# Cross attention: two of eight head pairs masked behind the exponentials by GpSimd

## The chip, the core and the metric

The kernel runs on one core of a Trainium2 chip. The metric is the device time of one launch in microseconds (us). The engines are called TensorE (PE in the rows), VectorE (DVE), ScalarE (ACT), GpSimd (POOL) and SyncE (SP, which here only issues transfers).

## The reference

A decoder layer on a batch of 128 sequences with 128 tokens of 256 features: self attention, cross attention over a context of the same shape, and a feed-forward part, each with a layer norm before it and a residual. Both attentions have 16 heads of 16 features. What the change touches is the mask of the cross attention:

```python
scores = jnp.einsum('bhqd,bhkd->bhqk', Q, K) / jnp.sqrt(jnp.float32(D_K))
scores = jnp.where(mask == 0, jnp.float32(1e-09), scores)
attn = jax.nn.softmax(scores, axis=-1)
out = jnp.einsum('bhqk,bhkd->bhqd', attn, V)
```

The mask has ones and zeros for each pair of query and key and is the same for all sequences and heads. A masked key keeps a score of about zero, so it keeps a weight.

## The kernel before

**Jobs and slots.** The batch is cut into 32 groups of 4 sequences (512 tokens). Each group is a self job and later a cross job: 64 jobs. The first six are self jobs, then cross and self jobs alternate (26 of each), and the last six are cross jobs. The program is a row of slots. In slot n every engine works on several jobs at once, each at another stage: job n+2 is normalised, n+1 projected, job n (`s.max`) gets its row maxima and values, job n-1 (`s.exp`) its exponentials and weighted sums, and job n-2 (`s.out`) its output product. Two sets of buffers ("even", "odd") take turns. Inside a slot each engine's order is written out by hand, and semaphores alone join the engines. After the last slot the feed-forward stage runs over the same groups.

**The exponentials of a job.** The 16 heads are 8 pairs. For pair p, `shifted(p)` on TensorE writes the transposed scores less the row's maximum into `exp_bank`; `exps(p)` on ScalarE turns them into `prob` (128 x 1024). `weighted(qd)` on TensorE multiplies the `prob` of pairs 2qd and 2qd+1 with the values; `outputs(b, s.exp, qd)` on VectorE transposes the result, for cross jobs adds the masked keys' part `ue`, and divides by the sum. `prob` has three buffers.

**The mask.** For a cross job, `add_mask` puts a large negative number on the masked places: four matmuls of 512 columns start the bank, and the scores are added to them. It is used for the maxima (`scores(m)` into `score_bank`, `sh.maskB`) and for the exponentials (`shifted(p)`, `sh.maskBT`). So masked places have an exponential of zero, and their true share (score about zero) comes in as `ue`, from sums over the masked keys.

**Order around the change.** On TensorE a slot runs `tile(0..3)` (projections of the next job), `scores(0..7)`, `shifted(0..7)`, `weighted(0..3)`, `products` (output product of an earlier job), `values` and `turn_maxima`, interleaved. `shifted(p)` waits for `exps(p-1)`, since there is one `exp_bank`. `scores(m)` waits for `maximum(m-1)` on VectorE, since there is one `score_bank`. VectorE runs `tile` (the low parts of the projections), `maximum(0..7)`, `outputs(0..2)` and at the end `negate`, for which `turn_maxima` waits. `outputs(3)` falls into the next slot. GpSimd has `low_outputs`, `low_norm`, `residual` and `biased` in a slot, and `low_context` for a cross job; all are subtractions or additions in SBUF.

**Prepared weights.** The feed-forward weights are made ternary and transposed at the start and stay in SBUF (`wfcT`, `wpT`).

## Time and profile before

| | |
|---|---|
| median of 3 runs | 2367.21 us (2365.73 to 2368.36) |
| the profiled execution | 2370.91 us |
| its span | 2369.1 us |
| TensorE busy | 2183.7 us, 92% |
| VectorE busy | 1933.5 us, 82% |
| ScalarE busy | 1596.8 us, 67% |
| GpSimd busy | 1044.4 us, 44% |
| chain that ended last, by engine | TensorE 65%, VectorE 18%, ScalarE 7%, issue 7% |

The span is the time from the first to the last instruction in one profiled execution; its own time lies 1.8 us above it and 3.7 us above the median. Busy shares are means over stages with different limits. The chain is followed back from the last instruction, at each step to what released it.

### The profile page before, as it was taken

Reading aid. Unit: us, or ns where it says so; the run is one execution under the profiler, and the core shown is the slowest. Engines: PE = TensorE matmul, PEld = TensorE weight load, DVE = VectorE, ACT = ScalarE, POOL = GpSimd, SP = SyncE. Lnnn points to the kernel's source line nnn. Section 1 sums busy time; section 2 is a strip of 40 time slices with the busy share of each in tenths; the row PEclk is TensorE's granted clock in tenths of the full one; section 3 lists DMA queues with packets and bytes.
Section 4 is the critical chain, followed back from the end, with each engine's and each line's share of the span. In section 5 each row is a group of like instructions: output and inputs, shape, how many; then the busy total and the mean of one; then the engine's idle time right before and its main releaser. Section 6 shows DMA issues by size and latency. Waiting matters only on the chain.

```text
span 2369.1 us, 70234 instructions
## 1 busy us (share of the span) xinstructions
PE 2183.7 (92%) x29033; PEld 1449.4 (61%) x29033; DVE 1933.5 (82%) x3903; ACT 1596.8 (67%) x2354; POOL 1044.4 (44%) x849
## 2 busy tenths in 40 slices
PE   4689999999999999999999999999967999999999
PEld 2356656656665666566566656655544777777776
DVE  5788888888888888888888888887745788887887
ACT  3377666667666666666666666665535878778786
POOL 2144443454444344444434444454224554555543
PEclk9799999999999999999999999999978999999999
DMA  4567666676666667666666766676422333333332
GB/s 129 117 151 175 156 144 155 145 158 157 157 153 152 155 140 159 157 160 153 154 150 143 153 161 157 159 173 144 89 59 54 84 103 80 97 89 83 103 81 63
DMA packets 472860, 311.01 MB, mean 131 GB/s; under 512 B 288144, under 2 KB 423184, under 8 KB 472592
## 3 DMA queue, kind: packets, MB, share of 16 engines
q1 hardware_dynamic: 469488, 306.80, 55.0%
q8 instruction: 205, 3.36, 0.6%
q10 hardware_dynamic: 3104, 0.34, 0.1%
q14 instruction: 63, 0.52, 0.1%
HBM read 71.65 MB, written 50.33 MB: 51 GB/s over the span
## 4 chain that ended last, share of the span: by engine, by line
PE 65%; DVE 18%; ACT 7%; issue 7%; SPq 1%; DMA 1%; POOL 1%; DVEq 0%; ACTq 0%; POOLq 0%
PE product_bank L1106 14%; PE ybk L1434 9%; PE hbk L1458 9%; PE out_bank L1082 7%; PE tbk L1448 5%; ACT prob L811 4%; PE product_bank L1113 4%; PE score_bank L1030 4%; DVE out_bank L940 4%; PE score_bank L1049 3%; DVE odd_mx L906 3%; PE exp_bank L1067 3%; PE exp_bank L1030 3%; PE exp_bank L1167 3%; DVE att L955 2%
## 5 line engine op out<-in xcount | busy, mean ns | idle before, releaser
L811 ACT ACTIVATE prob<-exp_bank 128x1024 f32<-128x1024 f32 x512 | 523.1, 1022 | 254.6 <-PE exp_bank L1067 246.6
L735 POOL TENSOR_TENSOR xs<-xn,xs 128x1024 f16<-128x1024 f32 x64 | 136.3, 2130 | 638.8 <-ACT xs L835 638.8
L906 DVE TENSOR_REDUCE even_mx<-score_bank 128x8 f32<-128x1024 f32 x256 | 310.5, 1213 | 97.4 <-PE score_bank L1049 97.4
L906 DVE TENSOR_REDUCE odd_mx<-score_bank 128x8 f32<-128x1024 f32 x256 | 310.2, 1212 | 81.0 <-PE score_bank L1049 81.0
L801 ACT ACTIVATE qk<-product_bank,bcol 128x512 f16<-128x512 f32 x256 | 175.9, 687 | 232.0 <-PE product_bank L1106 228.7
L1458 PE MATMUL hbk<-wfcT,ffn_xhl 128*128 128x512 f16 x1024 | 264.5, 382 | 6.3 <-ACT hid L1355 3.4
L1418 DVE SCALAR_TENSOR_TENSOR ghl<-tbk,lnwc,ghl 128x512 f16<-128x512 f32 x256 | 188.0, 735 | 100.3 <-ACT ghl L1349 100.3
L1434 PE MATMUL ybk<-wpT,ghl 128*128 128x256 f16 x2048 | 260.5, 273 | 0.8 <-DVE ffn_y L1403 0.7
L1434 PEld LDWEIGHTS ybk<-wpT,ghl 128*128 128x128 f16 x2048 | 197.8, 98 | 66.1 <-DVE ghl L1418 0.9
L1349 ACT ACTIVATE ghl<-tbk,lnwc 128x512 f16<-128x512 f32 x256 | 174.1, 681 | 68.1 <-PE tbk L1448 68.1
L940 DVE STREAM_TRANSPOSE out_bank<-out_bank 128x512 f32<-128x512 f32 x256 | 183.5, 717 | 24.8 <-PE out_bank L1082 24.7
L912 DVE SCALAR_TENSOR_TENSOR qk<-product_bank,bcol,qk 128x512 f16<-128x512 f32 x256 | 184.2, 740 | 22.4 <-ACT qk L801 22.4
L1030 PE MATMUL exp_bank<-maskBT,pick 64*128 64x512 bf16 x1024 | 156.5, 385 | 45.3 <-ACT prob L811 27.7
L1113 PE MATMUL product_bank<-WT,ahl 128*128 128x256 f16 x1536 | 192.9, 276 | 4.8 <-POOL ahl L735 4.8
L735 POOL TENSOR_TENSOR ahl<-attT,ahl 128x512 f16<-128x512 f32 x128 | 148.6, 1161 | 100.6 <-ACT ahl L816 100.6
L1379 DVE BATCH_NORM_STATS2 hstats<-hid 128x6 f32<-128x512 f32 x256 | 174.1, 680 | 16.5 <-ACT hid L1355 16.4
L1355 ACT ACTIVATE hid<-hbk 128x512 f32<-128x512 f32 x256 | 152.4, 596 | 51.0 <-PE hbk L1458 44.0
L1106 PE MATMUL product_bank<-odd_xhl,WT 128*128 128x512 f16 x732 | 176.0, 384 | 7.6 <-DVE qk L912 5.6
L1113 PEld LDWEIGHTS product_bank<-WT,ahl 128*128 128x128 f16 x1536 | 141.4, 99 | 34.3 <-POOL ahl L735 5.1
L1030 PE MATMUL score_bank<-maskB,pick 64*128 64x512 bf16 x1024 | 154.7, 381 | 6.3 <-DVE even_mx L906 5.6
L1448 PE MATMUL tbk<-ident,hid 128*128 128x128 f32 x1024 | 154.4, 274 | 0.7 <-ACT hid L1355 0.7
L1458 PEld LDWEIGHTS hbk<-wfcT,ffn_xhl 128*128 128x128 f16 x1024 | 98.2, 98 | 75.1 <-ACT hid L1355 5.2
(174 smaller groups left out, 4401.3 us busy)
## 6 DMA issues: line engine op xcount, KB each, us to landing
even_stk<-qk SPq DMA_DIRECT2D x384, 128.0 KB, 2.7
odd_stk<-qk SPq DMA_DIRECT2D x384, 128.0 KB, 2.8
x_scratch<-xn SPq DMA_DIRECT2D x64, 512.0 KB, 4.8
ctx_in<-in_ctx SPq DMA_DIRECT2D x32, 512.0 KB, 4.6
ffn_src<-x_scratch SPq DMA_DIRECT2D x32, 512.0 KB, 3.8
out<-ffn_y SPq DMA_DIRECT2D x32, 512.0 KB, 3.7
odd_src<-in_x SPq DMA_DIRECT2D x29, 512.0 KB, 5.4
even_src<-x_scratch SPq DMA_DIRECT2D x29, 512.0 KB, 5.5
```

The costliest lines, as they stand in the source:

```text
L735: nc.gpsimd.tensor_tensor(out, src, hi, ALU.subtract).then_inc(lo_ready, 1)
L811: act.activation(prob[:, p % 3], ebank[:, :, :], ACT.Exp, scale=EXP_SCALE).then_inc(b.exp_done, 1)
L906: dve.tensor_reduce(a.mx[:, g * H:(g + 1) * H].rearrange("p (r e j) -> p r e j", r=2, e=2)[:, :, eight], sbank[:, :, :].rearrange("p r (j ...
L912: dve.scalar_tensor_tensor(qk[:, 3 * (n // 2), n % 2], pbank[:, n % 2], sh.bcol[:, 2 * s.proj.which + n // 2, n % 2:n % 2 + 1], qk[:, 1 + ...
L940: dve.transpose(obank[:, 1], obank[:, 0]).then_inc(ch.o_turned, 1)
L1030: pe.matmul(bank[:, r].rearrange("p (b s) -> p b s", b=G), sh.pick[rows, h], mask[rows, h].unsqueeze(1).broadcast_to([HALF, G, S]), start= ...
L1106: last = pe.matmul(pbank[:, n % 2].rearrange("p (b s) -> p b s", b=G), sh.WT[:, (s.proj.wq, s.proj.wk)[n // 2], wp, kt, n % 2 * P:(n % 2 + ...
L1113: last = pe.matmul(pbank[:, g // 2, g % 2 * D:(g % 2 + 1) * D], stationary(part, g, kt), sh.WT[:, w, wp, kt, :], start=(k == 0 and kt == 0 ...
L1418: dve.scalar_tensor_tensor(ghl[:, LO, s], tbk[:, TURN_BANK[s]], sh.lnwc[:, s:s + 1], ghl[:, HI, s], ALU.mult, ALU.subtract).then_inc(glo_r ...
L1434: last = pe.matmul(ybk[:, b], ghl[:, part, t, b * S:(b + 1) * S], sh.wpT[:, t], start=(t == 0 and part == HI and b % 2 == 0), stop=(t == F ...
L1448: last = pe.transpose(tbk[:, TURN_BANK[s], b * S:(b + 1) * S], hid[:, 1 - half, b, s * P:(s + 1) * P], sh.ident[:, :])
L1458: last = pe.matmul(hbk[:, s % 2], xhl[:, half, part, s // 2, kt], sh.wfcT[:, kt, s % 2 * HF:(s % 2 + 1) * HF], start=(part == HI and kt == ...
```

## The change

For cross jobs, pairs 0 and 2 (`KEPT`) get no mask on TensorE. ScalarE takes the exponential of all their scores. GpSimd then bounds `prob` above by 3e38 (a masked score may lie over the maximum of the others, and its exponential may overflow) and multiplies it with `keepT`, a table of zeros and ones. `weighted(qd)` also waits for this (`kept`). `prob` gets a fourth buffer, so `exps(4)` and `exps(6)` wait for a weighted sum where `exps(3)`, `exps(5)` and `exps(7)` did.

In slots whose exponentials are of a cross job, `weighted(0)` moves behind `products(0, 1)`, `weighted(1)` behind `products(2, 3)`, and on VectorE `maximum(4)` goes before the outputs of quad 0.

To make room in SBUF, `wfcT` and `wpT` are written to DRAM at the start and read again before the feed-forward stage. Some semaphores of the setup are merged, so that some waits ask for one transfer more.

```diff
+LARGE = 3e38
+KEPT = (0, 2)
...
+        def store_made(sp):
+            sp.wait_ge(fc_out, 2)
+            sp.dma_start(wfc_dram, wfcT[:, :, :].rearrange("p k f -> p (k f)")).then_inc(made_stored, 16)
+            sp.wait_ge(pj_out, 4)
+            sp.dma_start(wp_dram, wpT[:, :, :].rearrange("p t d -> p (t d)")).then_inc(made_stored, 16)
+            sp.wait_ge(made_stored, 32)
...
+            nc.vector.tensor_scalar(sh.keepT[:, :], bank[:, 5, 0:S], -1.0, 1.0, ALU.mult, ALU.add)
...
-        prob = sb("prob", [P, 3, 2, T])
+        prob = sb("prob", [P, 4, 2, T])
...
+            def keep_unmasked(p):
+
+                if s.exp and s.exp.cross and p in KEPT:
+                    pool.wait_ge(b.exp_done, 8 * s.exp.k + p + 1)
+                    tile = prob[:, p % 4].rearrange("p r (b s) -> p (r b) s", s=S)
+                    nc.gpsimd.tensor_scalar(prob[:, p % 4], prob[:, p % 4], LARGE, None, ALU.min).then_inc(bounded, 1)
+                    pool.wait_ge(bounded, len(KEPT) * s.exp.g + KEPT.index(p) + 1)
+                    nc.gpsimd.tensor_tensor(tile, tile, sh.keepT[:, :].unsqueeze(1).broadcast_to([P, 2 * G, S]), ALU.mult).then_inc(kept, 1)
...
             low_outputs(a, s.out, 1)
+            for p in KEPT:
+                keep_unmasked(p)
             low_norm()
...
-                    if p > 2 and p % 2:
-                        act.wait_ge(b.pv_done, 4 * s.exp.k + (p - 3) // 2 + 1)
+                    if p > 3 and p % 2 == 0:
+                        act.wait_ge(b.pv_done, 4 * s.exp.k + (p - 4) // 2 + 1)
...
-            outputs(b, s.exp, 0)
-            maximum(4)
+            if s.exp and s.exp.cross:
+                maximum(4)
+                outputs(b, s.exp, 0)
+            else:
+                outputs(b, s.exp, 0)
+                maximum(4)
...
-                if s.exp.cross:
+                masked = s.exp.cross and p not in KEPT
+                if masked:
                     add_mask(ebank, sh.maskBT)
...
+                if s.exp.cross:
+                    pe.wait_ge(kept, len(KEPT) * s.exp.g + sum(1 for p in KEPT if p < 2 * qd + 2))
...
+            late = s.exp is not None and s.exp.cross
...
-            weighted(0)
+            if not late:
+                weighted(0)
             scores(3)
             shifted(3)
             products(0, 1)
+            if late:
+                weighted(0)
             scores(4)
             shifted(4)
-            weighted(1)
+            if not late:
+                weighted(1)
             scores(5)
             shifted(5)
             products(2, 3)
+            if late:
+                weighted(1)
...
+            sp.dma_start(wfcT[:, :, :].rearrange("p k f -> p (k f)"), wfc_dram).then_inc(made_loaded, 16)
+            sp.dma_start(wpT[:, :, :].rearrange("p t d -> p (t d)"), wp_dram).then_inc(made_loaded, 16)
```

TensorE in a slot with the exponentials of a cross job, from `weighted(0)` in the kernel before (`out_bank<-prob` is a weighted sum, `exp_bank<-maskBT` a mask, `product_bank<-WT,ahl` the products):

```order
L1082 MATMUL out_bank<-prob,even_vals 32x128 x16
L1049 MATMUL score_bank<-odd_stk 128x128 x8
L1030 MATMUL exp_bank<-maskBT,pick 128x512 x4
L1067 MATMUL exp_bank<-even_stk 128x128 x8
L1113 MATMUL product_bank<-WT,ahl 128x256 x12
L1049 MATMUL score_bank<-odd_stk 128x128 x8
L1030 MATMUL exp_bank<-maskBT,pick 128x512 x4
L1067 MATMUL exp_bank<-even_stk 128x128 x8
L1082 MATMUL out_bank<-prob,even_vals 32x128 x16
L1049 MATMUL score_bank<-odd_stk 128x128 x8
L1030 MATMUL exp_bank<-maskBT,pick 128x512 x4
L1067 MATMUL exp_bank<-even_stk 128x128 x8
```

The same place in the changed kernel, from the mask of pair 3 to `weighted(1)`:

```order
L1060 MATMUL exp_bank<-maskBT,pick 128x512 x4
L1098 MATMUL exp_bank<-even_stk 128x128 x8
L1146 MATMUL product_bank<-WT,ahl 128x256 x12
L1115 MATMUL out_bank<-prob,even_vals 32x128 x16
L1079 MATMUL score_bank<-odd_stk 128x128 x8
L1060 MATMUL exp_bank<-maskBT,pick 128x512 x4
L1098 MATMUL exp_bank<-even_stk 128x128 x8
L1079 MATMUL score_bank<-odd_stk 128x128 x8
L1060 MATMUL exp_bank<-maskBT,pick 128x512 x4
L1098 MATMUL exp_bank<-even_stk 128x128 x8
L1146 MATMUL product_bank<-WT,ahl 128x256 x12
L1115 MATMUL out_bank<-prob,even_vals 32x128 x16
```

Both weighted sums now stand behind the twelve product matmuls that followed them.

VectorE in the same slot, from maximum 3 in the kernel before (`odd_mx` is a maximum; the four operations from the transpose to `att` are the outputs of one quad):

```order
L906 TENSOR_REDUCE odd_mx<-score_bank 128x2x4
L940 STREAM_TRANSPOSE out_bank<-out_bank 128x512
L947 TENSOR_TENSOR out_bank<-out_bank,ue 128x16x17
L951 RECIPROCAL rec<-out_bank 128x16
L955 TENSOR_TENSOR att<-out_bank,rec 128x16x16
L906 TENSOR_REDUCE odd_mx<-score_bank 128x2x4 x2
L940 STREAM_TRANSPOSE out_bank<-out_bank 128x512
```

And in the changed kernel:

```order
L932 TENSOR_REDUCE odd_mx<-score_bank 128x2x4 x2
L966 STREAM_TRANSPOSE out_bank<-out_bank 128x512
L973 TENSOR_TENSOR out_bank<-out_bank,ue 128x16x17
L977 RECIPROCAL rec<-out_bank 128x16
L981 TENSOR_TENSOR att<-out_bank,rec 128x16x16
L932 TENSOR_REDUCE odd_mx<-score_bank 128x2x4
L966 STREAM_TRANSPOSE out_bank<-out_bank 128x512
```

Maximum 4 has moved ahead of the outputs of quad 0.

GpSimd in the same slot of the changed kernel:

```order
L750 TENSOR_TENSOR ahl<-attT,ahl 128x512
L786 TENSOR_SCALAR prob<-prob 128x1024
L788 TENSOR_TENSOR prob<-prob,keepT 128x1024
L786 TENSOR_SCALAR prob<-prob 128x1024
L788 TENSOR_TENSOR prob<-prob,keepT 128x1024
L750 TENSOR_TENSOR xs<-xn,xs 128x1024
```

The four operations on `prob` are new; the first and last row followed each other before.

## Rows read from the trace of the kernel before

**Rows 1.** Busy time by stretch, middle of attention: stretch, length, engines, clock, DMA
```profile
260.00:1500.00 1240.00, 1175.09 (x18483) 753.29 (x18486) 1070.41 (x1911) 846.17 (x1146) 556.89 (x456) 1.00 0.67 154
```

**Rows 2.** Timeline, TensorE, one cross slot: start, length, work, idle before
```profile
814.32 2.76 PE L1106 MATMUL product_bank<-even_xhl,WT 128*128 128x512 f16 x12
...
819.74 1.47 PE L1106 MATMUL product_bank<-ctx_hl,WT 128*128 128x512 f16 x6
...
823.09 0.61 PE L1030 MATMUL exp_bank<-maskBT,pick 64*128 64x512 bf16 x4 [0.90 <-ACT prob L811]
823.53 0.39 PE L1067 MATMUL exp_bank<-even_stk 64*128 64x128 f16 x8
823.85 1.08 PE L1082 MATMUL out_bank<-prob,even_vals 128*32 128x128 f32 x32
824.86 0.40 PE L1049 MATMUL score_bank<-odd_stk 64*128 64x128 f16 x8
...
825.85 1.48 PE L1113 MATMUL product_bank<-WT,ahl 128*128 128x256 f16 x12
827.26 0.40 PE L1049 MATMUL score_bank<-odd_stk 64*128 64x128 f16 x8
...
829.59 0.40 PE L1049 MATMUL score_bank<-odd_stk 64*128 64x128 f16 x8 [0.26 <-DVE odd_mx L906]
...
830.57 1.48 PE L1113 MATMUL product_bank<-WT,ahl 128*128 128x256 f16 x12
831.99 0.61 PE L1030 MATMUL exp_bank<-maskBT,pick 64*128 64x512 bf16 x4
...
838.29 0.33 PE L1148 MATMUL score_bank<-ident,odd_negm 128*16 128x128 f16 x3 [0.42 <-DVE odd_negm L969]
```

**Rows 3.** Timeline, ScalarE, the same slot
```profile
819.68 1.02 ACT L811 ACTIVATE prob<-exp_bank 128x1024 f32<-128x1024 f32 x1
...
823.96 1.02 ACT L811 ACTIVATE prob<-exp_bank 128x1024 f32<-128x1024 f32 x1
...
828.36 1.02 ACT L811 ACTIVATE prob<-exp_bank 128x1024 f32<-128x1024 f32 x1 [1.31 <-PE exp_bank L1067]
```

**Rows 4.** Timeline, VectorE, the same slot
```profile
818.94 0.73 DVE L912 SCALAR_TENSOR_TENSOR qk<-product_bank,bcol,qk 128x512 f16<-128x512 f32 x1
...
825.30 1.23 DVE L906 TENSOR_REDUCE odd_mx<-score_bank 128x8 f32<-128x1024 f32 x1 [0.53 <-PE score_bank L1049]
826.44 0.72 DVE L940 STREAM_TRANSPOSE out_bank<-out_bank 128x512 f32<-128x512 f32 x1
...
828.32 1.21 DVE L906 TENSOR_REDUCE odd_mx<-score_bank 128x8 f32<-128x1024 f32 x1
...
831.17 0.72 DVE L940 STREAM_TRANSPOSE out_bank<-out_bank 128x512 f32<-128x512 f32 x1
...
838.01 0.23 DVE L969 TENSOR_TENSOR odd_negm<-odd_mx,mshift 128x64 f16<-128x64 f32 x1
```

**Rows 5.** Timeline, GpSimd, the same slot
```profile
830.40 2.13 POOL L735 TENSOR_TENSOR xs<-xn,xs 128x1024 f16<-128x1024 f32 x1 [10.59 <-ACT xs L835]
```

**Rows 6.** Groups by line and form: count, busy us, mean ns, idle before
```profile
L764 POOL TENSOR_TENSOR odd_xb<-odd_src,boB 128x1024 f32<-128x1024 f32 x32 | 76.0, 2375 | 72.4 <-DVE odd_negm L969 67.5 <-DVE odd_negm L967 4.9
...
L279 POOL TENSOR_SCALAR_AFFINE_SELECT ident<-ident 128x128 f32<-128x128 f32 x1 | 0.3, 297 | 0.2 <-POOL ones L276 0.2
```

**Rows 7.** DMA issues (count, size, us to landing), then SyncE's queue around slot 0
```profile
x_scratch<-xn SPq DMA_DIRECT2D x64, 512.0 KB, 4.8
...
78.51 0.37 SPq L1208 DMA_DIRECT2D ctx_in<-in_ctx  x1
85.89 2.57 SPq L660 DMA_DIRECT2D odd_stk<-qk  x4
```

**Rows 8.** Timeline, the last cross jobs: VectorE, then TensorE
```profile
1658.01 1.40 DVE L920 TENSOR_TENSOR ue<-ew,cntL 128x64 f32<-128x64 f32 x1
...
1661.28 2.25 PE L1106 MATMUL product_bank<-ctx_hl,WT 128*128 128x512 f16 x6 [1.83 <-DVE qk L912]
```

More of the change, by code:

```diff
@@ L67, in __init__ @@
         self.WT = sb("WT", [P, 8, 2, KT, D], F16)
-        self.wfcT = sb("wfcT", [P, KT, F], F16)
-        self.wpT = sb("wpT", [P, FT, D], F16)
         self.bcol = sb("bcol", [P, 4, KT])
@@ L85, in __init__ @@
         self.maskcT = sb("maskcT", [P, S])
+        self.keepT = sb("keepT", [P, S])
         self.cntL = sb("cntL", [P, BLOCKS])
@@ L110, in decoder_layer_kernel @@
         sh = Shared(sb)
-        prep = setup(nc, stack, ins, sh)
+        prep = setup(nc, stack, ins, sh, wfc_dram, wp_dram)
         att = attention(nc, stack, ins, sh, x1_dram, x2_dram, prep)
-        mlp = ffn(nc, stack, sh, x2_dram, out, att)
+        mlp = ffn(nc, stack, sh, x2_dram, out, att, wfc_dram, wp_dram)
         LAST = 2 * NG
@@ L397, in ternary @@
             dve.wait_ge(total_done, 1)
-            nc.vector.tensor_scalar(thr[:, :], bank[:, 0, 0:2], 1.0 / (F * D), GAMMA_EPS, ALU.mult, ALU.add).then_inc(gamma_done, 1)
-            dve.wait_ge(gamma_done, 1)
+            nc.vector.tensor_scalar(thr[:, :], bank[:, 0, 0:2], 1.0 / (F * D), GAMMA_EPS, ALU.mult, ALU.add).then_inc(thr_done, 1)
+            dve.wait_ge(thr_done, 1)
             nc.vector.tensor_scalar(nthr[:, :], thr[:, :], -0.5, None, ALU.mult).then_inc(thr_done, 1)
-            dve.wait_ge(thr_done, 1)
+            dve.wait_ge(thr_done, 2)
             nc.vector.tensor_scalar(thr[:, :], thr[:, :], 0.5, None, ALU.mult).then_inc(thr_done, 1)
-            dve.wait_ge(thr_done, 2)
+            dve.wait_ge(thr_done, 3)
             for n in range(2):
-                wait(dve, tern_done, n)
-                nc.vector.tensor_scalar(neg[:, :], fnat[:, n], nthr[:, n:n + 1], None, ALU.is_lt).then_inc(neg_done, 1)
-                dve.wait_ge(neg_done, n + 1)
+                wait(dve, tern_done, 2 * n)
+                nc.vector.tensor_scalar(neg[:, :], fnat[:, n], nthr[:, n:n + 1], None, ALU.is_lt).then_inc(tern_done, 1)
+                dve.wait_ge(tern_done, 2 * n + 1)
                 nc.vector.scalar_tensor_tensor(fnat[:, n], fnat[:, n], thr[:, n:n + 1], neg[:, :],
@@ L1067, in shifted @@
                         last = pe.matmul(ebank[:, r, g * S:(g + 1) * S], b.stk[rows, s.exp.k % 2, 1, p % 4, p // 4, g * S:(g + 1) * S],
-                                         b.stk[rows, s.exp.k % 2, 0, p % 4, p // 4, g * S:(g + 1) * S], start=not s.exp.cross, stop=True, skip_group_check=True)
+                                         b.stk[rows, s.exp.k % 2, 0, p % 4, p // 4, g * S:(g + 1) * S], start=not masked, stop=True, skip_group_check=True)
                 last.then_inc(b.st_mm, 1)
@@ L1226, in attention, with ffn @@
         return part
-def ffn(nc, program, sh, x2_dram, out, before):
+def ffn(nc, program, sh, x2_dram, out, before, wfc_dram, wp_dram):
     x2_groups = x2_dram.rearrange("(n b) s d -> n s b d", b=G)
@@ L1260, in ffn @@
         held = sb("ffn_held_wait", [P, 2, G + 1])
+        wfcT = sb("wfcT", [P, KT, F], F16)
+        wpT = sb("wpT", [P, FT, D], F16)
         hbk = ps("hbk", [P, 2, HF])
@@ L1433, in second @@
                     for part in (HI, LO):
-                        last = pe.matmul(ybk[:, b], ghl[:, part, t, b * S:(b + 1) * S], sh.wpT[:, t],
+                        last = pe.matmul(ybk[:, b], ghl[:, part, t, b * S:(b + 1) * S], wpT[:, t],
                                          start=(t == 0 and part == HI and b % 2 == 0), stop=(t == FT - 1 and part == LO),
@@ L1454, in pe_body @@
                             pe.wait_ge(x_turned, 16 * (k + 1))
+                            if isinstance(k, int) and k == 0:
+                                pe.wait_ge(made_loaded, 32)
                         wait(pe, hid_ready, 8 * k + s - 1)
```

49 lines of the change are left out of this document (28 added, 21 removed).

## Prediction

> **What bounds the kernel now.** I read the views in this order: busy time by stretch, to find the stage; the timeline of one slot of it, engine by engine, to find which wait ends last; then the groups and transfers that price what is new. In the middle of attention TensorE works 1175.09 of 1240 us at full clock, while GpSimd works 556.89 [rows 1]. So a reader could expect every removed matmul to come off the time. The slot's timeline says otherwise. I take the slot that runs the exponentials of a cross-attention job (TensorE from 814.32 [rows 2]) and write "at 823.09" for a time in that trace. Three places matter.
>
> First, ScalarE sets the pace of the early pairs. Scores of pair 2 start at 823.09, after a wait of 0.90 us for the exponential of pair 1 [rows 2]. The exponential of pair 2 then starts at 823.96, directly behind two batches of the layer norm, not behind TensorE [rows 3]. Second, TensorE fills ScalarE's time with the weighted sums: `weighted(0)` at 823.85 stands between the scores of pair 2 and those that wait for its exponential [rows 2]. Third, from 828.32 VectorE has little room: maximum 4, maximum 5, outputs 1 (at 831.17), the turn, maximum 6, outputs 2, maximum 7, and the negated maxima at 838.01 [rows 4]. TensorE stands 0.42 us for these before it turns the maxima at 838.29 [rows 2], and the next slot follows directly. The end of a slot hangs on VectorE's row of work, and the head of that row hangs on `weighted(1)`.
>
> **The masks removed.** Two of eight pairs lose four matmuls each, 64 groups in 32 jobs. A group delays what stands behind it by 0.44 us (823.09 to 823.53) [rows 2], so 28 us of TensorE's time go. What of that is on the path? Pair 0: behind its scores comes the third projection group at 819.74, which waits for VectorE's correction from 818.94 to 819.67 [rows 2, 4]; nothing of that correction waits for pair 0. Gain 0. Pair 2: its scores end 0.44 us sooner, but the exponential stays at 823.96 behind ScalarE's layer norm [rows 3]. It ends at 824.98, and the scores of pair 3 wait for it as before. Gain 0 there too; TensorE only waits longer.
>
> **The weighted sums and maximum moved.** Up to 825.85, where `products(0, 1)` start [rows 2], both kernels stand alike, except that `weighted(0)` is still to do. It costs 1.01 us (823.85 to 824.86). I walk on from there, with the distances of these rows:
> - `weighted(0)` starts at 827.26 and the next scores at 828.27, 1.01 later than before. The exponential of pair 4 starts at 829.37 instead of 828.36 [rows 2, 3] and ends at 830.39.
> - Maximum 4 starts 0.44 behind its scores (824.86 to 825.30) [rows 2, 4]: 828.71, and ends at 829.93 (before: 829.53). Scores 5 go to 830.00 (before 829.59).
> - Pair 5 waits for the exponential of pair 4: 830.45. Mask and scores take 0.76 (823.09 to 823.85): `products(2, 3)` start at 831.21 instead of 830.57, take 1.42 (to 831.99), and only then comes `weighted(1)`, from 832.63 to 833.71. Pair 6 is 1.65 late.
> - VectorE did outputs 0 from 826.44 to 828.32 [rows 4], in time in which it had nothing else. Now they stand behind maximum 4: 829.86 to 831.74. Maximum 5 ends at 832.95. Outputs 1 need `weighted(1)` and start at 833.84, not at 831.17: 2.67 late.
> - From there the row is as dense as before (831.17 to 838.01 is 6.84 [rows 4]). The negated maxima come at 840.68 and the turn of the maxima at 840.96 instead of 838.29.
>
> So each such slot is 2.67 us longer by this walk. Other distances of the next slot start from this turn (the maxima go by a transfer into the scores), so I count no recovery; I take 2.6, since the joints are rounded upward. Its bounds are 1.65 (TensorE's own delay, if VectorE makes up the rest) and 2.67. Of 32 cross jobs 26 alternate with self jobs: 26 x 2.6 = 67.6. The last six follow each other in slots with more idle time, for which no row answers directly; between 0 and 2.67 each I take 1.0, nearer to 0 because VectorE waits there for scores as well. That makes 6.0.
>
> **GpSimd's new work.** The product with a broadcast table is like the residual with a broadcast bias, 2.375 us [rows 6]. No row shows a one-input operation on 1024 elements. The two ends are 1.7 (the select of 128 elements, 0.297 us, less about 0.1 of start, times eight [rows 6]) and 2.38 (as if it had two inputs). I take 1.7, the one-input row: 4.1 a pair. Pair 0's exponential runs 819.68 to 820.70 [rows 3], so it is masked at 824.8, needed at 827.26. Pair 2 is masked at 829.1, needed at 832.63. GpSimd's next work in the slot is not due before the layer norm's split, 830.40 [rows 5]. With 2.38 they come at 825.5 and 830.2. Cost 0 in either case; what hides it is the very delay of the weighted sums.
>
> The Trainium skill, "GPSIMD Engine Reference", section "Engine selection", advises VectorE for elementwise work and calls GpSimd about line-rate for one input; from its 1.2 GHz the minimum would be an estimated 0.9 us, and the sum would stay the same. No row of this trace shows that rate.
>
> **The rest.** Both prepared feed-forward weights (512 KB each) are stored before slot 0 and loaded again before the feed-forward stage. The stores go ahead of the context load at 78.51; with about 0.6 us each to issue and 4.8 to land the queue is free near 84.5, before its next transfer at 85.89 [rows 7]. Cost 0, up to 5 if they land later. The loads are issued behind the first two groups' loads, some 40 us before they are needed; cost 0, up to 4 if they slow those. One more copy of 128 columns on VectorE: 0.3, in the noise. The fourth buffer for exponentials frees ScalarE sooner, but ScalarE never waited for a buffer in these rows: 0. Merged semaphores wait for transfers that have landed: 0.
>
> **Sum.** 67.6 + 6.0 = 73.6 us. The profiled execution took 2370.91 us with a span of 2369.1; the median of the runs is 2367.21. The walk gives a difference, so I add it to the median: 2440.8, about 2441 us. The likeliest case alone runs from 26 x 1.65 = 43 (2410) to 32 x 2.67 = 85 (2453).
>
> **Rivals.**
> - *GpSimd becomes the bound.* Both pairs must be masked between 820.75 and 832.63, so a pair may take 5.9 us. From a minimum of 3.5 us on, `weighted(1)` waits for GpSimd. At 4.5 the pairs take 13.8 and each job loses a further 1.9: 2441 + 32 x 1.9 = 2502. Against it: twice the two-input price is needed. One row speaks for trouble between the two engines: a VectorE product of 64 columns took 1.40 us at 1658.01 [rows 8] beside GpSimd's work. The Trainium skill, "SBUF — State Buffer", section "Who interferes with whom", says that this hits VectorE instructions with two SBUF inputs; in the stretch where GpSimd now works VectorE has none, so by that rule nothing is added.
> - *The clock falls in the new waits.* At 1661.28, after an idle 1.83 us, six projection matmuls took 2.25 us [rows 8] against 1.47 at 819.74 [rows 2]: half clock. Two groups' worth is 1.6 us; in 32 slots 51 us: 2492. It decides once waits come near 1.83; the longest in my walk is 1.2. The Trainium skill, "TensorE: Matmul & The Clock Gate", part 1, has the clock fall to 1.2 GHz after idleness; that would be this case.
> - *Faster.* If outputs 1 can start by about 831.2 in spite of the order (because the exponentials of the early pairs come sooner than I read, so that `weighted(1)` isn't late), TensorE's 28 us come off: 2339. For it: TensorE is 95% busy [rows 1]. Against it: the fixed order and ScalarE's layer norm at 823.96.
> - *No change.* The self job's slot makes up what the cross job's loses, since each engine idles somewhere in it: 2367. Against it: its start hangs on the turn of the maxima.
>
> **How the numbers follow.** Likeliest case 0.78, GpSimd the bound 0.06, clock 0.04, faster 0.08, no change 0.04. Slower by over 0.2% (about what a measurement of this kernel can tell) is 0.88, within 0.04, faster 0.08. The range 2410 to 2495 holds nearly all of the likeliest case, the clock's case and the milder half of GpSimd's, about 0.83; "faster" and "no change" stay out.
>
> **What would show it.** Right: slots of cross jobs 2.6 us longer and unchanged slots of self jobs; the exponential of pair 2 as soon after that of pair 1 as now; outputs 1 waiting for `weighted(1)`; a TensorE that waits for the exponential of pair 2 over 1 us with nothing to fill it; GpSimd's pairs at 4 us with slack. Wrong: `weighted(1)` waiting for GpSimd, a granted clock under 1.0 in the steady stretch, or a VectorE that reaches the negated maxima no later than now.

## Result and the profile after

The changed kernel takes 2448.28 us (median of 4 runs, 2446.42 to 2450.37), the kernel before 2367.78 us beside it (2365.73 to 2368.45). The ratio is 1.0336, with a 95% interval of 1.032 to 1.0351: 80.5 us slower, where the prediction had 73.6. The span of the profiled execution grew from 2369.1 to 2445.3 us.

| | before | after |
|---|---|---|
| TensorE busy | 2183.7 us, 92% | 2173.7 us, 89% |
| VectorE busy | 1933.5 us, 82% | 1930.4 us, 79% |
| ScalarE busy | 1596.8 us, 67% | 1591.4 us, 65% |
| GpSimd busy | 1044.4 us, 44% | 1372.3 us, 56% |
| chain that ended last | TensorE 65%, VectorE 18%, ScalarE 7%, issue 7% | TensorE 63%, VectorE 19%, ScalarE 9%, issue 5% |

No engine became fuller but GpSimd, and it is far from full. The work of the others is spread over more time. Busy time by stretch shows it for the middle of attention (stretch, length, TensorE, its weight loads, VectorE, ScalarE, GpSimd, granted clock, DMA share, GB/s), where [rows 1] had 1175.09 for TensorE:

```profile
260.00:1500.00 1240.00, 1116.66 (x17473) 711.38 (x17477) 1019.05 (x1827) 802.88 (x1091) 758.64 (x521) 1.00 0.63 146
```

The clock is 1.00, so TensorE idles. One cross slot tells where. Its timeline on TensorE after the change (start, length, what, idle before it) answers to [rows 2]; the slot begins at 900.52, so 86.20 is to be taken off to compare it with the one that began at 814.32:

```profile
900.52 2.76 PE L1139 MATMUL product_bank<-even_xhl,WT 128*128 128x512 f16 x12
...
909.29 0.40 PE L1098 MATMUL exp_bank<-even_stk 64*128 64x128 f16 x8 [0.90 <-ACT prob L837]
...
911.18 0.60 PE L1060 MATMUL exp_bank<-maskBT,pick 64*128 64x512 bf16 x4 [1.06 <-ACT prob L837]
...
911.94 1.49 PE L1146 MATMUL product_bank<-WT,ahl 128*128 128x256 f16 x12
913.36 1.08 PE L1115 MATMUL out_bank<-prob,even_vals 128*32 128x128 f32 x32
914.37 0.40 PE L1079 MATMUL score_bank<-odd_stk 64*128 64x128 f16 x8
...
916.09 0.40 PE L1079 MATMUL score_bank<-odd_stk 64*128 64x128 f16 x8 [0.67 <-DVE odd_mx L932]
...
917.36 1.48 PE L1146 MATMUL product_bank<-WT,ahl 128*128 128x256 f16 x12
918.78 1.08 PE L1115 MATMUL out_bank<-prob,even_vals 128*32 128x128 f32 x32
...
927.13 0.33 PE L1181 MATMUL score_bank<-ident,odd_negm 128*16 128x128 f16 x3 [0.79 <-DVE odd_negm L995]
```

TensorE now stands twice for ScalarE, 0.90 and 1.06 us, since nothing fills the second wait: `weighted(0)`, which did, comes at 913.36 only, behind `products(0, 1)`. `weighted(1)` comes at 918.78, behind `products(2, 3)`. VectorE's timeline in the same slot answers to [rows 4]: maximum 3, maximum 4, outputs 0, maximum 5, outputs 1, negated maxima:

```profile
910.89 1.22 DVE L932 TENSOR_REDUCE odd_mx<-score_bank 128x8 f32<-128x1024 f32 x1
914.81 1.23 DVE L932 TENSOR_REDUCE odd_mx<-score_bank 128x8 f32<-128x1024 f32 x1 [2.70 <-PE score_bank L1079]
915.95 0.72 DVE L966 STREAM_TRANSPOSE out_bank<-out_bank 128x512 f32<-128x512 f32 x1
...
917.82 1.22 DVE L932 TENSOR_REDUCE odd_mx<-score_bank 128x8 f32<-128x1024 f32 x1
920.00 0.73 DVE L966 STREAM_TRANSPOSE out_bank<-out_bank 128x512 f32<-128x512 f32 x1 [0.96 <-PE out_bank L1115]
...
926.85 0.23 DVE L995 TENSOR_TENSOR odd_negm<-odd_mx,mshift 128x64 f16<-128x64 f32 x1
```

VectorE idles 2.70 us for scores 4, and 0.96 us more before outputs 1, for `weighted(1)`. Then it works without a gap to the negated maxima, as before. The next slot starts on TensorE at 928.33. So this cross slot has 27.81 us, the one before the change 25.16; a self slot has 26.79 us now and 26.84 before.

GpSimd's timeline in the slot: the minimum (L786) and the product (L788) of pair 0, then of pair 2, then the split that [rows 5] showed at 830.40:

```profile
906.75 2.77 POOL L786 TENSOR_SCALAR prob<-prob 128x1024 f32<-128x1024 f32 x1 [0.74 <-ACT prob L837]
909.61 2.35 POOL L788 TENSOR_TENSOR prob<-prob,keepT 128x1024 f32<-128x1024 f32 x1
911.93 2.77 POOL L786 TENSOR_SCALAR prob<-prob 128x1024 f32<-128x1024 f32 x1
914.78 2.35 POOL L788 TENSOR_TENSOR prob<-prob,keepT 128x1024 f32<-128x1024 f32 x1
917.57 2.14 POOL L750 TENSOR_TENSOR xs<-xn,xs 128x1024 f16<-128x1024 f32 x1 [0.43 <-ACT xs L861]
```

Pair 0 is ready at 911.96, 1.40 us before `weighted(0)`, and pair 2 at 917.13, 1.65 us before `weighted(1)`. No row of TensorE waits for GpSimd here.

### The profile page after: what moved, and what is told of

Read it like the earlier page. It is cut to its first block, busy times and chain, and to the rows that moved or that the text cites. A ratio compares the mean times of both kernels' runs of the same rounds, so it can differ in the third digit from the quotient of the medians.

```text
span 2445.3 us, 69793 instructions
## 1 busy us (share of the span) xinstructions
PE 2173.7 (89%) x28777; PEld 1437.4 (59%) x28777; DVE 1930.4 (79%) x3904; ACT 1591.4 (65%) x2354; POOL 1372.3 (56%) x977
## 4 chain that ended last, share of the span: by engine, by line
PE 63%; DVE 19%; ACT 9%; issue 5%; DMA 2%; SPq 1%; POOL 1%; DVEq 0%; ACTq 0%; POOLq 0%
PE product_bank L1139 11%; PE ybk L1477 9%; PE hbk L1503 9%; PE product_bank L1146 7%; PE out_bank L1115 7%; ACT prob L837 5%; PE tbk L1491 5%; DVE odd_mx L932 4%; PE score_bank L1060 4%; PE exp_bank L1098 3%; DVE out_bank L966 3%; PE exp_bank L1060 3%; PE exp_bank L1200 2%; PE score_bank L1079 2%; DVE even_mx L932 2%
## 5 line engine op out<-in xcount | busy, mean ns | idle before, releaser
L932 DVE TENSOR_REDUCE odd_mx<-score_bank 128x8 f32<-128x1024 f32 x256 | 309.7, 1210 | 130.4 <-PE score_bank L1079 130.3
L932 DVE TENSOR_REDUCE even_mx<-score_bank 128x8 f32<-128x1024 f32 x256 | 310.6, 1213 | 99.9 <-PE score_bank L1079 99.9
L786 POOL TENSOR_SCALAR prob<-prob 128x1024 f32<-128x1024 f32 x64 | 177.2, 2769 | 23.4 <-ACT prob L837 23.3
L1369 POOL TENSOR_TENSOR ffn_xs<-ffn_xn,ffn_xs 128x1024 f16<-128x1024 f32 x32 | 68.3, 2134 | 169.1 <-ACT ffn_xs L1409 169.1
```

The costliest lines, as they stand in the source:

```text
L932: dve.tensor_reduce(a.mx[:, g * H:(g + 1) * H].rearrange("p (r e j) -> p r e j", r=2, e=2)[:, :, eight], sbank[:, :, :].rearrange("p r (j ...
```

## The experiments

The theory on trial is the prediction's: the masks are worth nothing here, GpSimd is hidden, and the order alone (weighted sums behind products, and through them VectorE's row) costs the time. Its rivals: GpSimd or its port costs it; the masks were worth much and something else ate it; the clock. All kernels are made from the changed one. The table collects the results; the difference is the ratio's, against the kernel before on the same chip, and a cross slot is the distance on TensorE's timeline from the projection group that opens it to the one that opens the next. The self slots have 26.8 us in each of these kernels. Where cross slots of one kernel differ, the column says so: the longer ones hold matmuls at half clock, of which more below.

| kernel | median, us | ratio, 95% | difference, us | cross slot, us |
|---|---|---|---|---|
| before | 2367.78 | 1 | 0 | 25.16 |
| changed | 2448.28 | 1.0336 (1.032 to 1.0351) | +80.5 | 27.81 |
| order alone | 2452.25 | 1.0351 (1.0334 to 1.0368) | +82.6 | 27.87, in 2 of 26 29.5 |
| base: neither order nor GpSimd | 2368.52 | 0.9997 (0.9987 to 1.0007) | -1.1 | 25.17 |
| order, pairs 0 and 2 unmasked | 2448.62 | 1.0337 (1.032 to 1.0354) | +79.0 | 27.80 |
| old order, pairs 0 and 2 unmasked | 2354.92 | 0.9941 (0.9925 to 0.9958) | -14.7 | 24.73 |
| base, maximum 4 first | 2405.45 | 1.0165 (1.0144 to 1.0185) | +36.1 | 26.30 |
| base, weighted sum 1 late | 2432.01 | 1.0272 (1.0253 to 1.029) | +62.6 | 27.21 |
| base, weighted sum 0 late | 2438.03 | 1.0298 (1.028 to 1.0316) | +69.2 | 27.17, in 6 of 26 28.8 |
| changed, maximum 4 back | 2525.26 | 1.0655 (1.0639 to 1.0671) | +156.5 | 29.15 in 4 of 26, the others 30.6 and more |
| GpSimd's masking in the old order | 2473.18 | 1.0438 (1.0417 to 1.046) | +103.8 | 28.2 to 29.7 |
| changed, second minimum for pair 2 | 2488.28 | 1.0503 (1.0487 to 1.052) | +119.5 | 29.10, in 12 of 26 29.4 |
| old order, product alone for pair 2 | 2355.75 | 0.9945 (0.9926 to 0.9964) | -13.6 | 24.73 |
| base, scores 3 first | 2357.52 | 0.9959 (0.9945 to 0.9972) | -11.3 | 24.84 |

### Order alone, and neither

TensorE masks all eight pairs again, GpSimd nothing; the order of the change stays:

```diff
-KEPT = (0, 2)
+KEPT = ()
...
-                if s.exp.cross:
-                    pe.wait_ge(kept, len(KEPT) * s.exp.g + sum(1 for p in KEPT if p < 2 * qd + 2))
```

> The changed kernel with TensorE masking all eight pairs again and GpSimd masking none; its order of the weighted sums, of products and of the maximum of score bank 4 stays. Theory (the order costs it all, through maximum 4 ahead of outputs 0 and the weighted sum 1 behind products 2,3): 2446 to 2453 us, the cross slot at 27.8 us. Rival (the masks that left TensorE or the work that came to GpSimd make up the difference): within 10 us of the kernel before, 2357 to 2377. Halfway values would mean that both count.

It took 2452.25 us. The whole loss is there with every mask back on TensorE and GpSimd as before, so neither the mask's removal nor GpSimd's work makes it. Then the order goes back as well:

```diff
-            late = s.exp is not None and s.exp.cross
+            late = False
...
-            if s.exp and s.exp.cross:
-                maximum(4)
-                outputs(b, s.exp, 0)
-            else:
-                outputs(b, s.exp, 0)
-                maximum(4)
+            outputs(b, s.exp, 0)
+            maximum(4)
```

> The changed kernel with all that belongs to the masking undone: TensorE masks all eight pairs, GpSimd none, order of before. What stays are four probability buffers, the two weight matrices of the feed-forward stage stored to DRAM and loaded again, and the merged semaphores of the setup. Theory (stores and loads lie beside other work): 2366 to 2371 us. Rival (they cost what their bounds allowed): up to 2376.

2368.52 us, a ratio of 0.9997 whose interval includes 1. The trip of two weight matrices through DRAM, the fourth buffer and the setup's merged waits cost nothing that can be measured.

### What the masks and GpSimd are worth in each order

In the next kernel the order of the change stays and GpSimd's two operations and the wait for them are gone:

```diff
-            for p in KEPT:
-                keep_unmasked(p)
...
-                if s.exp.cross:
-                    pe.wait_ge(kept, len(KEPT) * s.exp.g + sum(1 for p in KEPT if p < 2 * qd + 2))
```

> The changed kernel, order and masks as in it, without GpSimd's minimum and product and without the wait for them: head pairs 0 and 2 stay unmasked. Theory (GpSimd is hidden, 1.65 us ahead of need): as the changed kernel, 2444 to 2450 us. Rival (GpSimd delays the weighted sums or takes time from VectorE): more than 10 us under it, below 2438.

2448.62 us, the time of the changed kernel: GpSimd's 328 us of work cost nothing that the runs can tell. Beside the order alone (2452.25) it also prices the two masks in this order: 3.6 us by the medians, with intervals that overlap, and 0.07 us a cross slot, 1.8 us in 26, by the timelines. The timeline of the order alone shows why they are worth so little there. These are TensorE's masks of pairs 2 and 3 and the products behind them:

```profile
801.90 0.61 PE L1060 MATMUL exp_bank<-maskBT,pick 64*128 64x512 bf16 x4 [0.90 <-ACT prob L837]
...
803.85 0.61 PE L1060 MATMUL exp_bank<-maskBT,pick 64*128 64x512 bf16 x4 [0.90 <-ACT prob L837]
...
804.62 1.48 PE L1144 MATMUL product_bank<-WT,ahl 128*128 128x256 f16 x12
```

TensorE waits for ScalarE before both. From pair 2 to the mask of pair 3 are 1.95 us; in the changed kernel, which has no mask for pair 2, they are 1.89 (909.29 to 911.18) with a wait of 1.06 in place of 0.90. ScalarE sets the pace, as the exponentials of pairs 2 and 3 in the changed kernel say:

```profile
910.12 1.01 ACT L837 ACTIVATE prob<-exp_bank 128x1024 f32<-128x1024 f32 x1
911.02 1.08 ACT L850 ACTIVATE xn<-odd_src,odd_nmr,odd_rstd 128x256 f32<-128x256 f32 x2
912.05 1.03 ACT L837 ACTIVATE prob<-exp_bank 128x1024 f32<-128x1024 f32 x1
```

The same two masks left out in the old order (base, with pairs 0 and 2 unmasked and nothing from GpSimd):

> The kernel before's order with the masks of head pairs 0 and 2 left out and nothing in their place: these two pairs are not masked. It prices the gain that the change could have had at most. Theory of the prediction (pair 0 waits for VectorE's correction, pair 2 for ScalarE, both gain 0): 2360 to 2370 us. Weaker form, in which pair 2's shorter group in front of scores 3 lets the chain of maxima start earlier: 0.4 us in each of 26 cross slots, 2355 to 2360. Rival (each mask is 0.44 us of TensorE on the path, 28 us in all): 2339.

2354.92 us: 14.7 us faster, 0.1 us under the range of the weaker form and half of the rival's gain. TensorE's timeline at pair 2 (unmasked), `weighted(0)`, scores 3, and the mask of pair 3 (this slot begins at 812.81, so 1.51 is to be added to compare it with the one at 814.32):

```profile
821.57 0.40 PE L1092 MATMUL exp_bank<-even_stk 64*128 64x128 f16 x8 [0.90 <-ACT prob L835]
821.90 1.08 PE L1107 MATMUL out_bank<-prob,even_vals 128*32 128x128 f32 x32
822.91 0.40 PE L1073 MATMUL score_bank<-odd_stk 64*128 64x128 f16 x8
823.46 0.61 PE L1054 MATMUL exp_bank<-maskBT,pick 64*128 64x512 bf16 x4 [0.15 <-ACT prob L835]
```

The mask of pair 3 gains little: TensorE waits 0.15 us for it here, where in the kernel before its row shows no wait and stands 0.12 us behind the end of the exponential of pair 2 (824.98):

```profile
825.10 0.59 PE L1030 MATMUL exp_bank<-maskBT,pick 64*128 64x512 bf16 x4
```

That mask comes 0.13 us sooner. Scores 3, which stand ahead of it, come 0.44 us sooner (822.91 for 824.86), and maximum 3, which in [rows 4] waited 0.53 us for them, does so too (823.35 for 825.30):

```profile
823.35 1.23 DVE L930 TENSOR_REDUCE odd_mx<-score_bank 128x8 f32<-128x1024 f32 x1
```

VectorE's row behind it keeps the 0.44 us (maximum 4 at 826.37 for 828.32), and the slot ends 0.43 us sooner: 24.73 us for 25.16, 11.2 us in 26 slots. This is the weaker form of the theory, which named this way. It is one mask of two; pair 0 gives nothing, as foretold, for the kernel with pair 2 alone, below, has the same slot. The new order closed the gain off: in it scores 3 stand ahead of `weighted(0)`, and maximum 3 waits for VectorE's own corrections and not for them (910.89 above, without a wait).

### Which move costs

Each move by itself, on the base (TensorE masks all pairs, GpSimd none). First VectorE's: maximum 4 ahead of outputs 0.

```diff
-            outputs(b, s.exp, 0)
-            maximum(4)
+            if s.exp and s.exp.cross:
+                maximum(4)
+                outputs(b, s.exp, 0)
+            else:
+                outputs(b, s.exp, 0)
+                maximum(4)
```

> The kernel of e_base (TensorE masks all, order of before) with one move: VectorE's maximum of score bank 4 ahead of outputs 0 in the cross slots. By the timeline of before, weighted sum 0 ends at 824.93 and scores 4 at 825.26, so maximum 4 could begin at 825.30 and end at 826.51, and outputs 0 begins 1.2 us later than before: product (2,3) and the copies of its outputs are not urgent by that much, but turned outputs 0 are waited for by weighted sum 1 on TensorE (it began at 828.24, outputs 0 ended at about 827.1 and would now end at 828.4). Theory A (a small cost, the weighted sums 1 wait 0.1 to 0.5 us): 2370 to 2385 us. Theory B (the maxima come later by a full 1.2 us in each of 32 slots): 2405 and more. Rival C (maxima earlier, a gain): below 2364.

2405.45 us and 1.1 us a slot: the size of theory B, by the wait that theory A had named and taken for 0.1 to 0.5 us. It stands in TensorE's row of `weighted(1)`, with VectorE's transposition of outputs 0, which it waits for, above it:

```profile
841.02 0.72 DVE L966 STREAM_TRANSPOSE out_bank<-out_bank 128x512 f32<-128x512 f32 x1
```

```profile
841.89 1.08 PE L1113 MATMUL out_bank<-prob,even_vals 128*32 128x128 f32 x32 [1.40 <-DVE out_bank L966]
```

The weighted sum overwrites the bank that the outputs are read from, so a late outputs 0 is a late `weighted(1)` on TensorE, and scores 5 and maximum 5 behind it are late as well (maximum 4 itself comes sooner). Next, `weighted(1)` behind `products(2, 3)`, where `late` puts it:

```diff
-            late = False
+            late = s.exp is not None and s.exp.cross
...
-            if not late:
-                weighted(0)
+            weighted(0)
             scores(3)
             shifted(3)
             products(0, 1)
-            if late:
-                weighted(0)
```

> The kernel of e_base with one move: weighted sum 1 behind products (2,3) and scores 5 in the cross slots; weighted sum 0 and the order of VectorE stay. Theory (VectorE takes outputs 1 between maxima 5 and 6, and gets them later by the 1.48 us of products (2,3); 1 to 1.5 us in each of 26 slots): 2395 to 2415 us. Rival (the two moves cost only together): 2366 to 2376.

2432.01 us, and 2.05 us a slot, more than I had put down. VectorE's row of outputs 1, 18.88 us into its slot and not 16.85 as in [rows 4]:

```profile
856.11 0.73 DVE L966 STREAM_TRANSPOSE out_bank<-out_bank 128x512 f32<-128x512 f32 x1 [1.95 <-PE out_bank L1109]
```

Beside the products a wait comes in: scores 5 stand for maximum 4, in the time that `weighted(1)` filled before (there 0.26 [rows 2]):

```profile
852.50 0.40 PE L1075 MATMUL score_bank<-odd_stk 64*128 64x128 f16 x8 [1.27 <-DVE odd_mx L932]
```

Third, `weighted(0)` behind `scores(3)` and `products(0, 1)`:

```diff
-            late = False
+            late = s.exp is not None and s.exp.cross
...
-            if not late:
-                weighted(1)
+            weighted(1)
             scores(5)
             shifted(5)
             products(2, 3)
-            if late:
-                weighted(1)
```

> The kernel of e_base with one move: weighted sum 0 behind scores 3 and products (0,1) in the cross slots; weighted sum 1 and VectorE's order stay. Theory (a weighted sum moved behind a pair of products makes outputs of it, and the maximum queued behind them on VectorE, late by the 1.4 us of the products, as the move of weighted sum 1 alone did with +62.6 us): 2415 to 2435. Rival (it is the earlier one of the two and scores 3 gain what it loses, so that it costs little): under 2385. If the three moves were independent, this one would cost 82.6 - 62.6 - 36 = -16 us, 2353.

2438.03 us, 3 above the range. Again VectorE stands still, at outputs 0 (first row), with maximum 4 queued behind it, and TensorE's scores 5 wait for that maximum (second fence):

```profile
854.22 0.73 DVE L966 STREAM_TRANSPOSE out_bank<-out_bank 128x512 f32<-128x512 f32 x1 [2.53 <-PE out_bank L1109]
```

```profile
857.38 0.40 PE L1075 MATMUL score_bank<-odd_stk 64*128 64x128 f16 x8 [1.20 <-DVE odd_mx L932]
```

In six of its 26 cross slots the products behind the second wait for ScalarE run at half clock (2.74 us for 1.48 at 905.82) and the slot has 28.8 us, so some 10 of its 69.2 us are the clock's.

Alone the three moves cost 36.1, 62.6 and 69.2 us, together 82.6, half the sum of 167.9. They overlap: with both sums late VectorE has free time before outputs 0, and maximum 4 uses it. The next kernel shows this from the other side. It is the changed kernel with `maximum(4)` behind `outputs(b, s.exp, 0)` again.

> The changed kernel with one move undone: VectorE's maximum of score bank 4 stands behind outputs 0 again, the weighted sums stay late, GpSimd masks as in the change. Theory (the move of the maximum, which alone cost 36 us, mends a part of what the late weighted sums cost: without it maximum 4 waits for outputs 0 of a late weighted sum 0): slower than the changed kernel by 1 to 1.5 us in each of 26 to 32 slots, 2475 to 2500 us. Rival (its cost adds to the others, undoing it gives back 36 us): 2412.

2525.26 us: the move of the maximum, a loss by itself, saves 76 us beside the late sums, more than the 27 to 52 expected. In the slot shown VectorE waits 4.03 us for `weighted(0)`, and scores 5 stand 2.32 us for the maximum behind it; the products before that sum took 2.74 us.

```profile
833.60 0.73 DVE L966 STREAM_TRANSPOSE out_bank<-out_bank 128x512 f32<-128x512 f32 x1 [4.03 <-PE out_bank L1111]
```

```profile
829.65 2.74 PE L1142 MATMUL product_bank<-WT,ahl 128*128 128x256 f16 x12
...
836.76 0.40 PE L1075 MATMUL score_bank<-odd_stk 64*128 64x128 f16 x8 [2.32 <-DVE odd_mx L932]
```

Half of the 76 us are the clock's. Busy time by stretch, first for a slot of 29.15 us, then for those products (the clock is third from the end):

```profile
534.00:563.00 29.00, 23.13 (x357) 14.66 (x356) 21.61 (x37) 17.28 (x24) 18.40 (x10) 1.00 0.45 114
829.50:832.50 3.00, 3.00 (x21) 1.83 (x20) 0.07 (x1) 1.09 (x2) 2.92 (x2) 0.50 0.77 206
```

Four of the 26 cross slots have 29.15 us, at a clock of 1.00: 1.34 more than in the changed kernel, 35 us in 26 slots, which is the size expected. The other 22 are longer by 1.4 to 3.1 us, 38 us together.

### What GpSimd would cost without the new order

The masking of the change with `late = False` and `maximum(4)` at its old place:

> The change's masking on GpSimd for head pairs 0 and 2 with the order of before: weighted sums, products and maxima as they stood. Then weighted sum 0 waits for GpSimd's product of pair 0 and weighted sum 1 for that of pair 2. By the durations in the trace of after (2.77 and 2.35 us, begun at once behind the exponential) pair 0 is ready 5.2 us after its exponential's end and pair 2 5.1 us after pair 0. In before weighted sum 0 begins 3.1 us after the exponential of pair 0 ends, so 2.2 us of wait; weighted sum 1 a further 4.4 us on, so 0.8 more. Theory: 2.2 to 3.2 us in each of some 30 slots, 2430 to 2465 us: the order of the change was no worse than the wait it avoids. Rival (the waits lie beside other waits, and the change would have been right in the old order): under 2400.

2473.18 us, above the range of the theory. `weighted(0)` waits 2.37 us, where 2.2 was foretold; the profile puts it down to the exponential, but that had long ended, and GpSimd's product of pair 0 ended at 810.79:

```profile
810.89 1.94 PE L1111 MATMUL out_bank<-prob,even_vals 128*32 128x128 f32 x32 [2.37 <-ACT prob L837]
```

Its 32 matmuls then take 1.94 us in place of 1.08. Busy time by stretch gives the clock (third from the end, 0.53):

```profile
811.00:814.50 3.50, 3.50 (x53) 2.45 (x53) 1.09 (x1) 0.00 (x0) 3.42 (x2) 0.53 0.75 192
```

So after that wait TensorE ran at 1.2 GHz, half its full clock, for nearly all of 3.5 us; over the middle of attention the granted clock is 0.96. The excess over the range goes with these matmuls: in the longest cross slots (29.4 to 29.7 us) the products behind the sum are slow as well (2.62 us for 1.48 at 426.25). `weighted(1)` doesn't wait for GpSimd. The new order is thus the lesser evil of the two: given the masking on GpSimd with both operations, it saves 23 us; but the masking itself is what makes it needed.

### How far GpSimd was from mattering

The changed kernel with the minimum of pair 2 done twice:

```diff
-                    nc.gpsimd.tensor_scalar(prob[:, p % 4], prob[:, p % 4], LARGE, None, ALU.min).then_inc(bounded, 1)
-                    pool.wait_ge(bounded, len(KEPT) * s.exp.g + KEPT.index(p) + 1)
+                    for again in range(1 + (p == 2)):
+                        nc.gpsimd.tensor_scalar(prob[:, p % 4], prob[:, p % 4], LARGE, None, ALU.min).then_inc(bounded, 1)
+                        pool.wait_ge(bounded, 3 * s.exp.g + KEPT.index(p) + again + 1)
```

> The changed kernel with GpSimd's minimum of head pair 2 done twice (the second changes nothing): 2.77 us more before pair 2 is ready in each cross slot. In the trace of after GpSimd has finished pair 2 1.65 us before weighted sum 1 begins. Theory (GpSimd is hidden by just that): 2.77 - 1.65 = 1.1 us of wait in each of 26 to 32 slots, 2475 to 2490 us. Rival (GpSimd counts in full): 72 to 89 us, 2520 to 2537. Rival (it does not matter at all): 2448.

2488.28 us, 39 more than the changed kernel by the ratios and inside the theory's range. GpSimd's rows (both minima in one row) and TensorE's `weighted(1)` in one of its cross slots:

```profile
872.19 5.62 POOL L787 TENSOR_SCALAR prob<-prob 128x1024 f32<-128x1024 f32 x2
877.89 2.35 POOL L789 TENSOR_TENSOR prob<-prob,keepT 128x1024 f32<-128x1024 f32 x1
```

```profile
880.34 1.08 PE L1116 MATMUL out_bank<-prob,even_vals 128*32 128x128 f32 x32 [1.23 <-issue]
```

The product ends at 880.24 and the sum starts at 880.34, 1.23 us late, where 2.77 - 1.65 = 1.1 was expected; the slot has 29.10 us, 1.29 more. In another slot, at 804.65, the loss is 1.56 us, of another kind: the products there take 2.74 us at a granted clock of 0.50, and `weighted(1)` then waits for nobody.

```profile
816.09 2.74 PE L1147 MATMUL product_bank<-WT,ahl 128*128 128x256 f16 x12
```

```profile
816.00:819.00 3.00, 3.00 (x26) 1.82 (x23) 0.24 (x1) 1.22 (x2) 2.92 (x3) 0.50 0.77 209
```

### Two kernels that are faster than both

The gain of 14.7 us belongs to pair 2, and `weighted(1)` in the old order starts 3.3 us after the end of that exponential (824.98 to 828.24; my 3.6 below was too much). One GpSimd operation fits in, two don't. So pair 2 alone is masked by the product alone. What is left out is the minimum, which bounds an exponential that overflowed; without it such a value times zero would not be zero.

```diff
-KEPT = (0, 2)
+KEPT = (2,)
...
-                    nc.gpsimd.tensor_scalar(prob[:, p % 4], prob[:, p % 4], LARGE, None, ALU.min).then_inc(bounded, 1)
-                    pool.wait_ge(bounded, len(KEPT) * s.exp.g + KEPT.index(p) + 1)
```

> Head pair 2 alone masked by GpSimd, with the product only (the minimum, which bounds an exponential that overflowed, is left out), in the order of before; TensorE masks the other seven. The product is ready 2.4 us after the exponential's end, and weighted sum 1 starts 3.6 us behind that in before. Theory (after e_masks_only: pair 2's mask, 0.43 us behind TensorE's wait for ScalarE, was on the path in each slot, pair 0's was not): 2354 to 2358 us, faster than the kernel before by 0.5 to 0.6%. Rival (the gain of e_masks_only came from pair 0): 2366 to 2370. Rival (GpSimd's product is too late or takes VectorE's port): above 2372.

2355.75 us, the slot again 24.73. GpSimd's product, and `weighted(1)` 0.8 us after its end:

```profile
822.86 2.37 POOL L786 TENSOR_TENSOR prob<-prob,keepT 128x1024 f32<-128x1024 f32 x1 [5.19 <-ACT prob L835]
```

```profile
826.00 1.08 PE L1109 MATMUL out_bank<-prob,even_vals 128*32 128x128 f32 x32
```

The last kernel leaves nothing out and has no work on GpSimd. It is the base with scores 3 ahead of `weighted(0)` in the cross slots in which a projection runs, the opposite of what the change did to the chain of maxima:

```diff
-            if not late:
-                weighted(0)
-            scores(3)
+            if s.exp is not None and s.exp.cross and s.proj is not None:
+                scores(3)
+            weighted(0)
+            if not (s.exp is not None and s.exp.cross and s.proj is not None):
+                scores(3)
```

> The kernel of e_base (TensorE masks all eight pairs, nothing left out) with one move the other way: in cross slots in which a projection runs, scores 3 stand ahead of weighted sum 0 instead of behind it. In before VectorE's maximum 3 waited 0.53 us for scores 3 (825.30), which TensorE began 1.01 us late for weighted sum 0. Theory (the chain through VectorE's maxima sets the slot): 0.4 to 0.5 us in each of 26 slots, 2355 to 2361 us. Rival (outputs 0 come later by the same and the maxima behind them give the gain back): 2366 to 2372. Rival (scores 4, released earlier, push shifted scores back and ScalarE's exponentials late): slower, 2375 and more.

2357.52 us, ratio 0.9959 (0.9945 to 0.9972), faster than both by a move of one line. Maximum 3 starts behind VectorE's two corrections without a wait, where [rows 4] had 0.53:

```profile
822.46 1.21 DVE L932 TENSOR_REDUCE odd_mx<-score_bank 128x8 f32<-128x1024 f32 x1
```

The slot gains 0.32 us, less than that 0.53: maximum 5 now waits for scores 5, which stand in TensorE's own full row. It and the product for pair 2 weren't tried together; both shorten the same wait of maximum 3.

## Why the prediction was right

**What bounds the kernel.** Right. The self slots stayed (26.84 and 26.79 us), the cross slots grew, and in each the end hangs on VectorE's row from outputs 1 on. From outputs 1 to the negated maxima are 6.85 us (920.00 to 926.85), where [rows 4] had 6.84.

**The walk.** It gave 2.67 us for a cross slot, of which 2.6 were taken; measured were 2.65. Its stations, with 86.20 added, against the rows:

| station | walk | after |
|---|---|---|
| `weighted(0)` | 913.46 | 913.36 |
| maximum 4 | 914.91 | 914.81 |
| scores 5 | 916.20 | 916.09 |
| `products(2, 3)` | 917.41 | 917.36 |
| `weighted(1)` | 918.83 | 918.78 |
| outputs 0 | 916.06 | 915.95 |
| outputs 1 | 920.04 | 920.00 |
| turn of the maxima | 927.16 | 927.13 |

Since the distances came from rows of the same kinds of work, each joint added only some hundredths. The single moves can't be priced so: they don't add up (168 us for 83), and the prediction was right to walk through them together. The sizes that I gave them one by one before those runs were too low each time (for maximum 4, in the theory put first).

**The masks removed.** Right in the sum, with a step left out. In the new order both gain nearly nothing (1.8 us by the timelines, 3.6 by the medians, for 28 us of matmuls). But the prediction gave pair 2 a gain of 0 because "the scores of pair 3 wait for it as before". That wait is not all that stands behind pair 2: scores 3 come between, and [rows 4] had maximum 3 waiting 0.53 us for them. So in the old order the mask of pair 2 was on the path through VectorE and worth 0.43 us a slot, though the mask of pair 3 gained only 0.13. The late `weighted(0)` is what took that away. A reader who had trusted the sentence would have missed the 14.7 us.

**GpSimd.** Hidden, as foretold, but the minimum was mis-sized. I took 1.7 us, by scaling a small one-input operation, with 2.38 as the upper end. The groups by line and form, after the change:

```profile
L786 POOL TENSOR_SCALAR prob<-prob 128x1024 f32<-128x1024 f32 x64 | 177.2, 2769 | 23.4 <-ACT prob L837 23.3
L788 POOL TENSOR_TENSOR prob<-prob,keepT 128x1024 f32<-128x1024 f32 x64 | 150.6, 2353 | 5.3
```

2.77 us is above both ends; the product's 2.35 fits its row of 2.375. So a pair takes 5.2 us of the 5.9 that it may take, not 4.1, and the slack was 1.65 us where the text had 3.5. The verdict held by less than it seemed, as the second minimum shows. The Trainium skill, "GPSIMD Engine Reference", section "Engine selection", calls one input "roughly line-rate"; the estimate of 0.9 us worked out from that is a third of what the trace has, and the measurement decides.

VectorE did not suffer beside GpSimd: its maxima over 1024 elements take a mean of 1210 and 1213 ns with GpSimd's new work and 1211 and 1213 in the kernel with the order alone, which has none of it; maxima 3 and 4 in the slot above, beside GpSimd's products, took 1.22 and 1.23. By the rule of "SBUF — State Buffer", section "Who interferes with whom" (the Trainium skill), that was to be expected, and the trace agrees.

**The clock.** The likeliest case held: 1.00 in the middle of attention. But the condition given for the rival, waits near 1.83 us, is too simple. With the minimum twice the clock fell to 0.50 in a slot whose waits before were 0.90 and 1.06, and did not in the next cross slot, with the same two waits. With the order alone it fell in two of 26 cross slots, once to 0.50 behind waits of 0.90 and 0.90 (from 1515.20 on). There the loss per fall was the 1.6 us that the rival had (29.44 for 27.87). That the changed kernel, with 0.90 and 1.06 in its cross slots, stayed at 1.00 was luck as far as the prediction goes: the 1.2 us of its walk was no proof against a fall.

**The rest of the sum.** The last six cross jobs cost 7.2 us by the starts of their exponentials, 6.0 were taken. Not in the sum are 3.2 us, 2.6 of them in the first self slots. The trace of the base, with the same stores and setup, is 1.8 us behind at the same place, so most of it needs neither the order nor GpSimd; the cause is not shown. After the last slot the feed-forward stage is 1.6 us shorter. So 26 x 2.59 (the pair of slots, from exponential to exponential) + 7.2 + 3.2 - 1.6 is 76.1, and the span grew by 76.2. The medians are 4.3 us further apart than the spans: the profiled execution of before lies above its median, that of after below it, and runs of one kernel differ by as much.

**Stores and loads.** Nothing of them shows in the time: the base is at 0.9997 (0.9987 to 1.0007).

**What the other cases got wrong.** "Faster" asked that outputs 1 should start as early as before; they came 2.63 us late. "No change" asked for a self slot that makes up for it; it has 0.05 us to give.

## What to carry to other kernels

Work that seems to be free to move, because its result is not needed yet, may be what lets another engine's hand-written row go on: here a weighted sum held two engines, through the outputs and the maximum queued behind them. Walk one period through all its rows at once and price moves together, for alone they cost twice what they cost in company. And before work is taken off an engine, look for everyone who waits for what stands behind that work, not only for that engine's own next wait: a mask of 0.44 us was worth 0.43 where VectorE's maximum waited for the scores behind it, and nearly nothing where that maximum had other work ahead of it.
